# Attention output transposed tile by tile, projection features split and value blocks cleared earlier, and half of one expert weight matrix requested earlier, in a Perceiver block with a mixture of experts

## Chip, cores and metric

The kernel runs on one core of a Trainium2 chip. It is one launch of a program written instruction by instruction for each engine, with semaphores between them. The metric is the device time of one execution in microseconds (us): 675.45 us as the median of 3 runs, from 672.86 to 676.87.

## What is computed

The reference takes 512 tokens (8 sequences of 64, width 512) through three sublayers, each added to x after a layer norm: cross attention to a context of 8 x 512 rows, a linear attention, and a mixture of 16 experts with a shared expert.

```python
x = x + xattn(layernorm(x), ctx, ctx, Wq, bq, Wk, bk, Wv, bv, Wo, bo)      # 16 heads of 32
x = x + attn(layernorm(x), w_qkv, proj_matrix, w_out, b_out)
x = x + ffn(layernorm(x), gate_w, Wg, Wu, Wd, Ws_g, Ws_u, Ws_d)

def attn(x, w_qkv, proj, w_out, b_out):                                    # linear attention
    q, k, v = heads(x @ w_qkv)
    q_proj = elu1(einsum('bhnd,hdf->bhnf', q, proj))                       # elu1(x) = x + 1 if x > 0 else exp(x)
    k_proj = elu1(einsum('bhnd,hdf->bhnf', k, proj))
    kv = einsum('bhnf,bhnd->bhfd', k_proj, v)
    z = 1 / (einsum('bhnf,bhf->bhn', q_proj, k_proj.sum(2)) + 1e-8)
    return merge(einsum('bhnf,bhfd->bhnd', q_proj, kv) * z) @ w_out + b_out

def ffn(h, gate_w, Wg, Wu, Wd, Ws_g, Ws_u, Ws_d):
    scores = softmax(einsum('bsd,ed->bse', h, gate_w)).transpose(0, 2, 1)
    topk_w, topk_idx = top_k(scores, 8)                                    # each expert takes 8 tokens of each sequence
    x_tok = h[topk_idx]
    eo = (gelu(x_tok @ Wg.T) * (x_tok @ Wu.T)) @ Wd.T * topk_w
    return scatter_add(eo, topk_idx) + (gelu(h @ Ws_g.T) * (h @ Ws_u.T)) @ Ws_d.T
```

## The kernel before

Every engine has its own list of instructions, written out in the functions `perceiver_block` defines for SP (the queue of loads), POOL, ACT, DVE and PE. An engine works its list in order; a wait on a semaphore holds back all that stands behind it on that engine. Tokens are in 4 tiles of 128 (`NT`), the width of 512 is in 4 tiles of 128 (`KT`).

**Cross attention** (to about 286 us in the profile) runs over the 8 sequences. Its last sequence overlaps with the output projection (`cross_residual`, L1354) and the layer norm of the linear attention. DVE adds the projection to x (L831), takes the statistics (L812, L813, L814), ACT takes the square root (`ln_std`, L527), DVE finishes with `xn_lin` (L824). ACT does these square roots between its copies of the transposed probabilities (`last_probs_T_out`, L637), in the order of its list. POOL meanwhile subtracts the high part of the weights from the raw ones (`weights_low`, L503: `wlv_lo`, later `wlk_lo`, `wlq_lo`) and clears the block-diagonal value tile `v_bd` (L507, L511).

**Linear attention** (about 286 to 374 us) first projects q, k and v (`qkv_project`, L1405), each product as three of a high and a low part. `proj_hi` (ACT, L680) and `proj_lo` (DVE, L986) are the same split of the feature matrix. The table `LIN_ORDER` then sets the order of all that follows on PE, ACT and DVE: "p" is a projection of q, "k" and "q" are features (L1427, L1433; exponent L689, relu L691, DVE L999), "kv" the products of L1444, and ("att", i, t) is half i of the attention output of token tile t (L1456), which DVE divides and stores in `att` (L1021 to L1027). The last four entries are

```python
        LIN_ORDER += [("att", 1, t) for t in range(NT)]
```

Then PE transposes all of `att` (L1465) into four banks, one for each of the 4 tiles of the width, and ACT copies two of them to `att_T` (L703), DVE the other two (L1035). PE multiplies by `w_out` (`residual`, L1354) when all four copies are there. Behind its copies ACT splits the router's weights and the first stripes of the shared expert (`gate_hi`, `ws_g_hi`, `ws_u_hi`, `ws_d_hi`), DVE subtracts (`gate_lo`, `ws_g_lo`, `ws_u_lo`, `ws_d_lo`, L1048 to L1045), and only then, in DVE's list, come the layer norms of the four tiles (`residual_ln`, L831 first).

**Mixture of experts** (from about 390 us): the router's scores are transposed to [16, 512] in PSUM, copied to SBUF (L1107), and DVE takes the 8 largest of each sequence (L1109) and their positions (L1112). These indices, spread by PE over all partitions (L1594), pick the tokens (L1606, `x_slot`). Then the 24 items of `ITEMS` follow: 16 experts and 8 stripes of the shared expert, in the pattern s, e, e, s, e, e. Each expert has 3 matrices of 2 MB: `w_g`, `w_u` (L1495) and `w_d` (L1532), in two buffers each. SP requests a matrix as soon as PE has used the one that is in its buffer (`expert_load`). `w_d1`, the buffer for the odd experts' down weights, lies over tiles of the routing (`xn_moe`, `spread_i`), so its first load waits for the last pick (`sp.wait_ge(slot_ps, 2 * KT)`).

## Time and profile before

| what | value |
|---|---|
| median of 3 runs | 675.45 us |
| profiled execution, its own time | 672.65 us |
| span of the profiled execution, first to last instruction | 669.5 us |
| mean granted TensorE clock | 0.997 |
| PE busy | 638.5 us, 95% of the span |
| DVE busy | 319.3 us, 48% |
| ACT busy | 254.6 us, 38% |
| POOL busy | 36.6 us, 5% |
| DMA, mean | 193 GB/s, 129.55 MB |

PE is the engine with the most work, but a matmul that is pipelined counts as busy to its modelled end, so the 95% are not all work at full rate. The 31 us that PE is not busy lie in a few places. The timeline names each: a row in it has its start, its length, the engine, the line, what is written and read, and in brackets how long the engine stood idle before the row and who released it.

### The profile page before, as it was taken

Reading aid. Unit: us, or ns where it says so; the run is one execution under the profiler, and the core shown is the slowest. Engines: PE = TensorE matmul, PEld = TensorE weight load, DVE = VectorE, ACT = ScalarE, POOL = GpSimd, SP = SyncE. Lnnn points to the kernel's source line nnn. Section 1 sums busy time; section 2 is a strip of 40 time slices with the busy share of each in tenths; the row PEclk is TensorE's granted clock in tenths of the full one; section 3 lists DMA queues with packets and bytes.
Section 4 is the critical chain, followed back from the end, with each engine's and each line's share of the span. In section 5 each row is a group of like instructions: output and inputs, shape, how many; then the busy total and the mean of one; then the engine's idle time right before and its main releaser. Section 6 shows DMA issues by size and latency. Waiting matters only on the chain.

```text
span 669.5 us, 10402 instructions
## 1 busy us (share of the span) xinstructions
PE 638.5 (95%) x4216; PEld 414.6 (62%) x4216; DVE 319.3 (48%) x646; ACT 254.6 (38%) x486; POOL 36.6 (5%) x38
## 2 busy tenths in 40 slices
PE   6989999999999999898999998999999999999997
PEld 5767777787878776576888565444444434443433
DVE  5964635445362626847778775323233232323123
ACT  5744635454454426437685252111121212211110
POOL 0300000000000002436000000000000000000000
PEclk9999999999999999999999998999999999999999
DMA  8111010110430000030319633989999999999972
GB/s 312 81 64 64 1 65 14 51 62 3 173 143 1 1 2 1 1 111 0 130 57 430 265 130 126 389 334 417 381 415 416 406 399 404 391 380 387 370 291 74
DMA packets 14347, 129.55 MB, mean 193 GB/s; under 512 B 2720, under 2 KB 2848, under 8 KB 6240
## 3 DMA queue, kind: packets, MB, share of 16 engines
q1 hardware_dynamic: 12576, 127.15, 48.7%
q10 hardware_dynamic: 1728, 1.77, 0.8%
q8 instruction: 33, 0.54, 0.3%
q14 instruction: 10, 0.08, 0.0%
HBM read 125.90 MB, written 1.05 MB: 190 GB/s over the span
## 4 chain that ended last, share of the span: by engine, by line
PE 78%; DVE 9%; DMA 5%; ACT 4%; issue 2%; ACTq 2%; SPq 1%; DVEq 0%
PE ps L1211 22%; PE ps L1495 14%; PE ps L1532 7%; PE ps L1505 5%; PE ps L1405 5%; DMA w_u<-in_wu 4%; PE ps L1281 4%; PE ps L1354 3%; PE ps L1545 3%; PE ps L1257 3%; PE ps L1292 2%; PE ps L1322 2%; PE ps L1444 2%; ACTq L396 2%; PE ps L1456 1%
## 5 line engine op out<-in xcount | busy, mean ns | idle before, releaser
L1495 PE MATMUL ps<-w_u,x_slot 128*64 128x512 f32 x256 | 58.1, 595 | 1.3 <-DMA w_u<-in_wu 1.3
L1532 PE MATMUL ps<-w_d,hid_T 128*64 128x512 f32 x256 | 58.2, 596 | 1.1 <-ACT hid_T L763 1.1
L1495 PE MATMUL ps<-w_g,x_slot 128*64 128x512 f32 x256 | 58.1, 595 | 0.8 <-ACT x_slot L779 0.8
L582 ACT ACTIVATE probs<-ps,neg_max 128x512 f32<-128x512 f32 x64 | 43.5, 688 | 39.1 <-DVE neg_max L898 39.1
L741 ACT ACTIVATE hid<-ps 128x512 f32<-128x512 f32 x24 | 14.4, 598 | 102.6 <-PE ps L1495 76.8
L1211 PE MATMUL ps<-wv_hi,ctx_hi 128*128 128x512 f32 x128 | 51.5, 403 | 0.0
L878 DVE COPY probs_T<-ps 128x512 f32<-128x512 f32 x28 | 19.4, 692 | 64.8 <-PE ps L1281 64.8
L1211 PE MATMUL ps<-wv_lo,ctx_hi 128*128 128x512 f32 x128 | 49.9, 390 | 0.0
L1211 PE MATMUL ps<-wv_hi,ctx_lo 128*128 128x512 f32 x128 | 49.8, 389 | 0.0
L898 DVE TENSOR_REDUCE neg_max<-ps 128x1 f32<-128x512 f32 x64 | 39.8, 684 | 18.4 <-PE ps L1257 18.3
L1073 DVE TENSOR_TENSOR hid<-hid,ps 128x512 f32<-128x512 f32 x24 | 16.5, 687 | 65.7 <-PE ps L1495 36.1
L1211 PE MATMUL ps<-ctx_hi,wk_hi 128*128 128x512 f32 x112 | 44.4, 396 | 0.4 <-ACT k_T L567 0.4
L1211 PE MATMUL ps<-ctx_lo,wk_hi 128*128 128x512 f32 x112 | 43.6, 390 | 0.0
L1211 PE MATMUL ps<-ctx_hi,wk_lo 128*128 128x512 f32 x112 | 43.6, 390 | 0.0
L567 ACT ACTIVATE k_T<-ps,bias_k 128x512 f32<-128x512 f32 x32 | 21.6, 688 | 48.8 <-PE ps L1211 48.8
L1532 PEld LDWEIGHTS ps<-w_d,hid_T 128*64 128x64 f32 x256 | 17.7, 137 | 35.7 <-issue 34.4
L1495 PEld LDWEIGHTS ps<-w_u,x_slot 128*64 128x64 f32 x256 | 18.1, 137 | 35.0 <-issue 33.0
L1495 PEld LDWEIGHTS ps<-w_g,x_slot 128*64 128x64 f32 x256 | 17.9, 137 | 35.3 <-issue 34.2
L758 ACT COPY x_slot<-ps 64x512 f32<-64x512 f32 x14 | 8.1, 580 | 76.6 <-PE ps L1532 76.6
L1211 PEld LDWEIGHTS ps<-wv_hi,ctx_hi 128*128 128x128 f32 x128 | 24.0, 188 | 15.9 <-issue 5.7
L891 DVE TENSOR_SCALAR probs<-probs,row_inv 128x512 f32<-128x512 f32 x64 | 31.2, 487 | 2.3
L1281 PE MATMUL ps<-ident,probs 128*128 128x128 f32 x256 | 31.0, 274 | 0.0
(248 smaller groups left out, 1194.2 us busy)
## 6 DMA issues: line engine op xcount, KB each, us to landing
w_u<-in_wu SPq DMA_DIRECT2D x16, 2048.0 KB, 15.5
w_d<-in_wd SPq DMA_DIRECT2D x16, 2048.0 KB, 11.9
w_g<-in_wg SPq DMA_DIRECT2D x16, 2048.0 KB, 13.0
ctx_raw<-in_ctx SPq DMA_DIRECT2D x7, 1024.0 KB, 4.7
w_qkv<-in_wqkv SPq DMA_DIRECT2D x1, 3072.0 KB, 15.1
ws_g<-in_wsg SPq DMA_DIRECT2D x1, 2048.0 KB, 7.7
ws_u<-in_wsu SPq DMA_DIRECT2D x1, 2048.0 KB, 7.6
ws_d<-in_wsd SPq DMA_DIRECT2D x1, 2048.0 KB, 21.0
```

Source lines behind the costliest of these rows:

```text
L567: act.activation(k_T[:, ht, :], bank(FIRST_K + ht if first else PROJ[ht % 2]), ACT.Identity, bias=bias_k[:, ht:ht + 1], scale=1.0).then_in ...
L582: act.activation(probs[:, p, :], bank(SCORE[p]), ACT.Exp, bias=neg_max[:, p:p + 1], scale=1.0, accum_out=row_sum[:, p:p + 1]).then_inc(exp ...
L891: dve.tensor_scalar(probs[:, p, :], probs[:, p, :], row_inv[:, p:p + 1], None, ALU.mult).then_inc(prob_done, 1)
L898: dve.tensor_reduce(neg_max[:, p:p + 1], bank(SCORE[p]), AX.X, ALU.max, negate=True).then_inc(max_done, 1)
L1211: ins = pe.matmul(dst, a(dt), c(dt), start=(dt == 0 and i == 0), stop=(dt == KT - 1 and i == 2))
L1257: ins = pe.matmul(ps[L * side:L * (side + 1), SCORE[2 * ht + j // 2], :], q_T[rows, ht, L * b:L * (b + 1)], k_T[rows, ht, :], start=True, ...
L1281: ins = pe.transpose(ps[:, TRANS[ht % 2][pr], P * st:P * (st + 1)], probs[:, 2 * ht + pr, P * st:P * (st + 1)], ident[:])
L1354: ins = pe.matmul(bank(RES_BANK[k][t]), rows_T[:, dt, P * t:P * (t + 1)], w[:, dt, :], start=(dt == 0), stop=(dt == KT - 1))
L1405: ins = pe.matmul(bank(qkv_bank(n)), a, c, start=(dt == 0 and i == 0), stop=(dt == KT - 1 and i == 2))
L1495: ins = pe.matmul(ps[64 * fh:64 * (fh + 1), dst, :], x_slot[:, e, dt, :], weights[e % 2][:, dt, BANK * fh:BANK * (fh + 1)], start=(dt == 0 ...
L1505: ins = pe.matmul(bank(dst), a, c[:, dt, :], start=(dt == 0 and j == 0), stop=(dt == KT - 1 and j == 2))
L1532: ins = pe.matmul(ps[64 * fh:64 * (fh + 1), 6 + side(n), :], hid_T[:, side(n), j, 64 * fh:64 * (fh + 1)], w_d[e % 2][:, KT * fh + j, :], s ...
```

## The change

There are six edits.

1. POOL clears `v_bd` ahead of the four `wlv_lo` subtractions, not behind them.
2. ACT and DVE split the feature matrix (`proj_hi`, `proj_lo`) ahead of the key halves, not behind them, and POOL adds the bias rows to x only when `proj_lo` is finished.
3. `att` is transposed tile by tile of the tokens. Three tiles go between and behind the last attention products, the fourth behind the first tile's product with `w_out`. ACT makes all four copies to `att_T`, DVE none, and a product with `w_out` waits for its own tile.
4. DVE takes the 8 largest and their positions from PSUM. The copy to SBUF is gone.
5. `spread_i` moves into the memory of `x_slot`. With it gone from there, the second half of `w_d1` is free earlier.
6. The load of the second expert's down weights is in two halves of 1 MB. The second half is requested right behind `w_u` of that expert, the first half after the wait for the picks.

```diff
+        first = ExitStack()
+        spread_i = sb(first, "spread_i", [P, E, SLOTS], F32R)
+        first.close()
         x_slot = sb(moe, "x_slot", [P, E, KT, SLOTS])
...
-        spread_i = sb(route, "spread_i", [P, E, SLOTS], F32R)
...
-        ATT_BANK = (0, 1, 2, 7)
+        ATT_BANK = (7, 2, 3, 5)
...
-        LIN_ORDER += [("att", 1, t) for t in range(NT)]
+        LIN_ORDER += [("att", 1, 0), ("att", 1, 1), ("T", 0, 0), ("att", 1, 2), ("T", 0, 1), ("att", 1, 3), ("T", 0, 2)]
...
             expert_load("u", 1)
+            sp.dma_start(w_d1[:, KT:], wd_d[1][:, KT:]).then_inc(wd_half_in, 16)
             sp.wait_ge(slot_ps, 2 * KT)
-            expert_load("d", 1)
+            sp.dma_start(w_d1[:, :KT], wd_d[1][:, :KT]).then_inc(wd_in[1], 16)
...
-            weights_low(range(4))
             pool.wait_ge(v_ps, B * NS)
             pool.memset(v_bd[:], 0.0).then_inc(vbd_zero, 1)
...
-            weights_low(range(4, 12))
+            weights_low(range(12))
             pool.wait_ge(rows_in, 32)
+            pool.wait_ge(proj_split, 2)
             add_row_bias(1, bout_rows)
...
             values_out(6)
-            for n in range(4):
-                heads_high(n, kl_halves, n)
-                qkv_high((8 + n,))
             act.wait_ge(proj_in, 64)
             for i in range(2):
                 act.activation(proj_hi[:, :, i, :], proj_twice[:], ACT.Identity,
                                scale=head_mask[:, i:i + 1]).then_inc(proj_hi_done, 1)
+            for n in range(4):
+                heads_high(n, kl_halves, n)
+                qkv_high((8 + n,))
             values_out(7)
...
-            for dt in (0, 2):
-                act.wait_ge(attT_ps, dt + 1)
-                act.copy(att_T[:, dt, :], bank(ATT_BANK[dt])).then_inc(attT_act, 1)
+            for t in range(NT):
+                act.wait_ge(attT_ps, t + 1)
+                act.copy(att_T[:, :, P * t:P * (t + 1)],
+                         bank(ATT_BANK[t]).rearrange("p (k c) -> p k c", k=KT)).then_inc(attT_done, 1)
...
-            for dt in (1, 3):
-                dve.wait_ge(attT_ps, dt + 1)
-                dve.tensor_copy(att_T[:, dt, :], bank(ATT_BANK[dt])).then_inc(attT_dve, 1)
...
-            link(dve.tensor_copy(score_T, ps[0:E, 7, :]))
+            scores = ps[0:E, 7, :]
             for b in range(B):
-                ins = dve.max(top_w[:, b, :], score_T[:, L * b:L * (b + 1)])
+                ins = dve.max(top_w[:, b, :], scores[:, L * b:L * (b + 1)])
             link(ins)
             for b in range(B):
-                ins = dve.max_index(top_i[:, b, :], top_w[:, b, :], score_T[:, L * b:L * (b + 1)])
+                ins = dve.max_index(top_i[:, b, :], top_w[:, b, :], scores[:, L * b:L * (b + 1)])
...
+            def att_transpose(t):
+                pe.wait_ge(att_done, NT + t + 1)
+                for dt in range(KT):
+                    ins = pe.transpose(ps[:, ATT_BANK[t], P * dt:P * (dt + 1)], att[:, t, P * dt:P * (dt + 1)], ident[:])
+                ins.then_inc(attT_ps, 1)
...
             for t in range(NT - 1):
+                pe.wait_ge(attT_done, t + 1)
                 residual(1, t, att_T, w_out)
+                if t == 0:
+                    att_transpose(NT - 1)
+            pe.wait_ge(attT_done, NT)
             moe_transpose(0)
```

DVE has the same exchange of `proj_lo` and the key halves as ACT has of `proj_hi`.

PE at the end of the linear attention, before. The row of `kv,q_feat` is the last attention product, `ident,att` are transposes, `w_out,att_T` is the output projection, `ident,xn_moe` transposes for the experts.

```order
L1456 MATMUL ps<-kv,q_feat 128x96 [waits feat_done,att_done,kv_done_dve,kv_done_act]
L1456 MATMUL ps<-kv,q_feat 128x96 x7
L1465 MATMUL ps<-ident,att 128x128 [waits att_done,feat_done]
L1465 MATMUL ps<-ident,att 128x128 x3
L1465 MATMUL ps<-ident,att 128x128 [waits att_done]
L1465 MATMUL ps<-ident,att 128x128 x3
L1465 MATMUL ps<-ident,att 128x128 [waits att_done]
L1465 MATMUL ps<-ident,att 128x128 x3
L1465 MATMUL ps<-ident,att 128x128 [waits att_done]
L1465 MATMUL ps<-ident,att 128x128 x3
L1354 MATMUL ps<-w_out,att_T 128x512 [waits wout_in,attT_dve,attT_act]
L1354 MATMUL ps<-w_out,att_T 128x512 x11
```

The same place in the changed kernel:

```order
L1417 MATMUL ps<-ident,att 128x128 [waits att_done]
L1417 MATMUL ps<-ident,att 128x128 x3
L1465 MATMUL ps<-kv,q_feat 128x96 [waits feat_done,att_done,kv_done_dve,kv_done_act]
L1465 MATMUL ps<-kv,q_feat 128x96 x7
L1417 MATMUL ps<-ident,att 128x128 [waits att_done]
L1417 MATMUL ps<-ident,att 128x128 x3
L1465 MATMUL ps<-kv,q_feat 128x96 [waits feat_done,att_done,kv_done_dve,kv_done_act]
L1465 MATMUL ps<-kv,q_feat 128x96 x7
L1417 MATMUL ps<-ident,att 128x128 [waits att_done]
L1417 MATMUL ps<-ident,att 128x128 x3
L1355 MATMUL ps<-w_out,att_T 128x512 [waits attT_done,wout_in]
L1355 MATMUL ps<-w_out,att_T 128x512 x3
```

The transposes of the first three tiles now stand between or right behind the attention products. Those of the fourth stand behind the 4 matmuls of the first `w_out` product.

ACT at the same place, before:

```order
L691 ACTIVATE relus<-ps 128x512
L703 COPY att_T<-ps 128x512 [waits attT_ps] x2
L719 CAST gate_hi<-gate 128x128 [waits gate_in]
L710 CAST ws_g_hi<-ws_g 128x512 [waits wsd_in,wsu_in,wsg_in]
L711 CAST ws_u_hi<-ws_u 128x512
L716 CAST ws_d_hi<-ws_d 128x512
L527 ACT_TABLE_LOAD
L527 ACTIVATE std<-var_eps 128x1 [waits stats_done] x2
```

and in the changed kernel:

```order
L694 ACTIVATE relus<-ps 128x512
L706 COPY att_T<-ps 128x4x128 [waits attT_ps] x4
L723 CAST gate_hi<-gate 128x128 [waits gate_in]
L714 CAST ws_g_hi<-ws_g 128x512 [waits wsd_in,wsu_in,wsg_in]
L715 CAST ws_u_hi<-ws_u 128x512
L720 CAST ws_d_hi<-ws_d 128x512
L530 ACT_TABLE_LOAD
L530 ACTIVATE std<-var_eps 128x1 [waits stats_done] x2
```

There are four copies instead of two, and `gate_hi` stands behind the fourth.

POOL from the end of the cross attention on, before:

```order
L503 TENSOR_TENSOR wlv_lo<-w_qkv,wlv_hi 128x512 [waits qkv_hi_done] x4
L507 MEMSET v_bd 128x6144 [waits v_ps]
L511 MEMSET v_bd 64x64 [waits vbd_zero]
L511 MEMSET v_bd 64x64
L503 TENSOR_TENSOR wlk_lo<-w_qkv,wlk_hi 128x4x128 [waits qkv_hi_done,vbd_zero]
L503 TENSOR_TENSOR wlk_lo<-w_qkv,wlk_hi 128x4x128 [waits qkv_hi_done] x3
L503 TENSOR_TENSOR wlq_lo<-w_qkv,wlq_hi 128x4x128 [waits qkv_hi_done] x4
L494 TENSOR_TENSOR x<-x,bout_rows 128x512 [waits xn_done,rows_in]
```

and in the changed kernel:

```order
L509 MEMSET v_bd 128x6144 [waits v_ps]
L513 MEMSET v_bd 64x64 [waits vbd_zero]
L513 MEMSET v_bd 64x64
L506 TENSOR_TENSOR wlv_lo<-w_qkv,wlv_hi 128x512 [waits qkv_hi_done,vbd_zero]
L506 TENSOR_TENSOR wlv_lo<-w_qkv,wlv_hi 128x512 [waits qkv_hi_done] x3
L506 TENSOR_TENSOR wlk_lo<-w_qkv,wlk_hi 128x4x128 [waits qkv_hi_done] x4
L506 TENSOR_TENSOR wlq_lo<-w_qkv,wlq_hi 128x4x128 [waits qkv_hi_done] x4
L497 TENSOR_TENSOR x<-x,bout_rows 128x512 [waits xn_done,proj_split,rows_in]
```

The large memset has changed places with the four `wlv_lo`, and the addition of the bias rows waits for `proj_split`.

## Rows read from the trace of the kernel before

**Rows 1.** Busy per stretch: us; PE, PEld, DVE, ACT, POOL; clock, DMA share, GB/s.

```profile
449.96:480.76 30.80, 30.80 (x142) 14.04 (x140) 8.70 (x13) 5.97 (x11) 0.00 (x0) 1.00 0.99 398
```

**Rows 2.** Waits of PE from 420 us on: total, times, longest.

```profile
PE ps L1495 <- DMA w_u<-in_wu: 1.3, 2, 1.1
```

**Rows 3.** Timeline of POOL, 262 to 320 us: start, length, what, idle before it.

```profile
263.89 4.95 POOL L503 TENSOR_TENSOR wlv_lo<-w_qkv,wlv_hi 128x512 fp32r<-128x512 f32 x4 [231.49 <-ACT wlv_hi L642]
268.77 5.26 POOL L507 MEMSET v_bd<- 128x6144 f32 x1
```

**Rows 4.** Timeline of DVE, 262 to 320 us.

```profile
269.27 5.03 DVE L824 TENSOR_SCALAR xn_lin<-x,mean_var,rstd 128x512 f32<-128x512 f32 x1
```

**Rows 5.** Timeline of ACT, 262 to 320 us.

```profile
276.07 0.20 ACT L527 ACTIVATE std<-var_eps 128x1 f32<-128x1 f32 x1 [4.97 <-DVE var_eps L814]
...
279.56 2.03 ACT L637 COPY probs_T<-ps 128x512 f32<-128x512 f32 x4
```

**Rows 6.** Timeline of PE, 262 to 320 us.

```profile
277.38 0.65 PE L1292 MATMUL ps<-probs_T,v_s 128*32 128x64 f32 x32 [2.07 <-ACT probs_T L637]
...
283.19 3.70 PE L1354 MATMUL ps<-w_o,o_T 128*128 128x512 f32 x8 [0.21 <-DVE o_T L883]
```

**Rows 7.** Timelines of DVE and POOL, 0 to 34 us.

```profile
25.03 0.55 DVE L824 TENSOR_SCALAR probs<-x,mean_var,rstd 128x512 f32<-128x512 f32 x1
25.50 5.77 DVE L926 TENSOR_TENSOR wq_lo<-o_T,wq_hi 128x512 fp32r<-128x512 f32 x4
25.74 6.66 POOL L494 TENSOR_TENSOR x<-x,bo_rows 128x512 f32<-128x512 f32 x4 [23.41 <-DVE probs L824]
```

**Rows 8.** Timeline of PE, the first features of the linear attention.

```profile
314.64 0.39 PE L1427 MATMUL ps<-proj_hi,kl_halves 128*128 128x256 f32 x1 [2.27 <-DVE proj_lo L986]
```

**Rows 9.** Timelines of ACT and DVE around the feature matrix's split.

```profile
298.49 1.19 ACT L649 CAST kl_halves<-ps 64x512 fp32r<-64x512 f32 x2 [2.21 <-PE ps L1405]
...
308.58 2.19 ACT L680 ACTIVATE proj_hi<-proj_twice,head_mask 128x1024 fp32r<-128x1024 f32 x2
310.35 4.24 DVE L986 SCALAR_TENSOR_TENSOR proj_lo<-proj_twice,head_mask,proj_hi 128x1024 fp32r<-128x1024 f32 x2
```

**Rows 10.** SP's loads of that matrix, in the timeline and by time to landing.

```profile
288.09 1.82 SPq L435 DMA_DIRECT2D proj_twice<-in_proj  x4
proj_twice<-in_proj SPq DMA_DIRECT2D x4, 128.0 KB, 3.7
```

**Rows 11.** Timeline of PE, end of the linear attention.

```profile
364.50 7.43 PE L1456 MATMUL ps<-kv,q_feat 128*128 128x96 f32 x64 [1.13 <-DVE q_feat L999]
375.37 10.54 PE L1354 MATMUL ps<-w_out,att_T 128*128 128x512 f32 x24 [1.21 <-ACT att_T L703]
```

**Rows 12.** Timeline of DVE, 360 to 412 us.

```profile
372.59 0.86 DVE L1027 TENSOR_TENSOR att<-ps,den_inv 64x256 f32<-64x256 f32 x2
...
376.90 0.69 DVE L1045 TENSOR_TENSOR ws_d_lo<-ws_d,ws_d_hi 128x512 fp32r<-128x512 f32 x1
379.15 0.69 DVE L831 TENSOR_TENSOR x<-ps,x 128x512 f32<-128x512 f32 x1 [1.56 <-PE ps L1354]
...
390.33 0.69 DVE L831 TENSOR_TENSOR x<-ps,x 128x512 f32<-128x512 f32 x1 [0.24 <-PE ps L1354]
```

**Rows 13.** Timeline of ACT, the copies of att_T.

```profile
373.87 1.07 ACT L703 COPY att_T<-ps 128x512 f32<-128x512 f32 x2 [10.64 <-PE ps L1465]
```

**Rows 14.** Timeline of DVE, the softmax of the router and the top 8.

```profile
398.05 0.23 DVE L1101 TENSOR_TENSOR logit<-ps,lmax 128x64 f32<-128x64 f32 x1
...
399.34 0.23 DVE L1105 TENSOR_TENSOR logit<-logit,linv 128x64 f32<-128x64 f32 x1
400.27 0.68 DVE L1107 COPY give<-ps 16x512 f32<-16x512 f32 x1 [0.70 <-PE ps L1588]
```

**Rows 15.** Busy per stretch, columns as in rows 1: the picking.

```profile
404.00:410.00 6.00, 4.87 (x22) 4.08 (x23) 4.14 (x7) 1.92 (x4) 0.00 (x0) 0.72 0.00 0
```

**Rows 16.** Busy per stretch, columns as in rows 1: the queue runs empty.

```profile
446.00:447.00 1.00, 1.00 (x8) 0.32 (x6) 0.00 (x0) 0.47 (x1) 0.00 (x0) 1.00 0.08 33
```

More of the change, by code:

```diff
@@ L268, in perceiver_block @@
         ctx_in, wqkv_in, wo_in, wout_in, rows_in = (sem(f"{n}_in") for n in ("ctx", "wqkv", "wo", "wout", "rows"))
-        proj_in, gate_in = sem("proj_in"), sem("gate_in")
+        proj_in, gate_in, wd_half_in = sem("proj_in"), sem("gate_in"), sem("wd_half_in")
         wg_in, wu_in, wd_in = ([sem(f"{n}_in{i}") for i in range(2)] for n in ("wg", "wu", "wd"))
@@ L295, in perceiver_block @@
         kv_ps, kv_done, att_ps, att_done = sem("kv_ps"), [sem("kv_done_act"), sem("kv_done_dve")], sem("att_ps"), sem("att_done")
-        attT_ps, attT_act, attT_dve = sem("attT_ps"), sem("attT_act"), sem("attT_dve")
+        attT_ps, attT_done = sem("attT_ps"), sem("attT_done")
         logit_ps, lsub_done, lexp_done, score_done = (
@@ L980, in _ @@
             values_out(6)
-            for n in range(4):
-                heads_low(n, kl_halves, n)
-            values_out(7)
             for i in range(2):
@@ L988, in _ @@
                                          op1=ALU.subtract).then_inc(proj_split, 1)
+            for n in range(4):
+                heads_low(n, kl_halves, n)
+            values_out(7)
             u = w = a = 0
@@ L1014, in _ @@
                     w += 1
-                else:
+                elif kind == "att":
                     dve.wait_ge(att_ps, a + 1)
@@ L1411, in _ @@
                     linear_transpose(NT - 1)
+            def att_transpose(t):
[3 more added lines that the diff above has]
+                ins.then_inc(attT_ps, 1)
             u = w = a = 0
             for kind, i, r in LIN_ORDER:
-                if kind == "p":
+                if kind == "T":
+                    att_transpose(r)
+                elif kind == "p":
                     qkv_project(i)
@@ L1460, in _ @@
                     a += 1
-            pe.wait_ge(feat_done, 32)
-            for t in range(NT):
-                pe.wait_ge(att_done, NT + t + 1)
-                for dt in range(KT):
-                    ins = pe.transpose(ps[:, ATT_BANK[dt], P * t:P * (t + 1)], att[:, t, P * dt:P * (dt + 1)], ident[:])
-                    if t == NT - 1:
-                        ins.then_inc(attT_ps, 1)
-            pe.wait_ge(attT_act, 2)
-            pe.wait_ge(attT_dve, 2)
             pe.wait_ge(wout_in, 16)
@@ L1529, in item_down @@
                     pe.wait_ge(wd_in[e % 2], 16 * (e // 2 + 1))
+                    if e == 1:
+                        pe.wait_ge(wd_half_in, 16)
                     for j in range(KT):
```

## Prediction

> **What bounds the kernel now.** I read the busy times by stretch first, then PE's waits, then the timelines around each edited line. In the expert stage PE and the load queue are both full: a pair of experts takes 30.80 us, all of it PE busy, at a DMA share of 0.99 [rows 1], and the loads that PE waits for cost it 1.3 us in all, 1.1 of it at the last `w_u` [rows 2]. All loads there are requested when PE frees a buffer, so if PE comes to the experts earlier, the queue does too. Hence a microsecond won on the path ahead of the experts is a microsecond at the end, and the question is what each edit does to PE's path between 262 and 412 us. There, edits touch four places: a stall of DVE behind POOL, PE's wait for the feature matrix, the change from linear attention to the experts, and the routing.
>
> The profiled execution took 672.65 us, 3.15 more than its span. The sum is made against it; the median of the three runs is 2.8 us higher, and I carry the difference over unchanged.
>
> **Clearing `v_bd` first.** DVE's `xn_lin` of tile 0 took 5.03 us [rows 4], where the same statement elsewhere takes 0.55 [rows 7]. It starts in POOL's 5.26 us memset and ends with it [rows 3]. So DVE is 4.48 late, tile 1's square root runs on ACT at 276.07 after 4.97 idle [rows 5], ACT's copies of the probabilities stand behind it in its list, and PE waits 2.07 for them [rows 6]. In the new order the memset, whose condition (the last values) holds before POOL's first row at 263.89, starts there at the latest and ends by 269.15, before `xn_lin` at 269.27. What runs beside `xn_lin` now are the four `wlv_lo`, 4.95/4 = 1.24 each [rows 3]. A DVE instruction beside such a subtraction is slowed too, but by one at a time: four and four of them alternate in 5.77 and 6.66 us [rows 7], so 0.2 to 1.2 us for each `xn_lin`, and DVE's tile 1 has 1.8 us to spare before ACT's copies are wanted. Followed on, tile 2 is no longer late either, ACT's four copies begin at 276.7 instead of 279.56 [rows 5], and the last `w_o` product starts at 280.5 instead of 283.19 [rows 6]. **Gain 2.7**; at least 2.07 if only the named wait goes, and 0 if the new neighbours hold DVE as long as the memset did (rival c). `wlv_lo` ends near 274.7 and is wanted at 283.6, so its move costs nothing.
>
> The Trainium skill (SBUF — State Buffer, "Who interferes with whom") says that VectorE and GpSimd share a port pair which one instruction holds alone until it ends, a GpSimd operation of any kind holding off a `tensor_scalar` in its two-port mode. By that rule the memset's stall goes, and `xn_lin` may meet at most one `wlv_lo`; rows 4 and 7 agree.
>
> **Splitting the feature matrix first.** PE stands 2.27 us for `proj_lo` at 314.64 [rows 8]. In the new place ACT's 2.19 us of `proj_hi` fit exactly into the 2.21 it stands idle ahead of the first key half at 298.49 [rows 9]. DVE's two `proj_lo` (4.24 together [rows 9], part of which I lay to POOL's bias rows running beside them, which now wait) begin 1.1 us after ACT and end by 300 to 301.6, against a first key half that DVE took at 299.1. It catches up in the 1.4 us gaps behind, and PE needs the key halves at 312 only. The matrix has landed: requested until 289.91, plus 3.7 us, is 293.6 [rows 10], wanted at 296.3. What is late next is ACT, which after its last q half loads the table of Exp; its first exponent comes only 0.5 us earlier, but PE has 12 matmuls of the next projection to do meanwhile. **Gain 2.25** (2.27 less a short wait at the fourth feature); ends 1.7 and 2.3. POOL's added wait delays nobody: the bias rows are wanted 60 us later.
>
> **Transposes by tile.** On PE alone this is a gain. Before, attention products run from 364.50 for 7.43, and the `w_out` products start at 375.37 after 1.21 of waiting [rows 11]. Now three transposes of 0.44 lie between them and the first `w_out` product starts at 373.2; the three products and the fourth transpose end at 384.0 instead of 385.7. But the chain that counts here is not PE's. ACT copies tile 3 only when PE has transposed it, and PE does that behind the first product (10.54/3 = 3.5 us [rows 11]): 373.2 + 3.5 + 0.6 = 377.3. Before, ACT's second copy began at 374.4 [rows 13]. All of ACT's splits stand behind that copy, and DVE's subtractions behind the splits: `ws_d_lo` ended at 377.59 [rows 12], 3.24 after the second copy began. Now it ends at 377.3 + 3.24 = 380.5. Only then may DVE start tile 0's layer norm, at 379.15 before [rows 12]. From there DVE works without a pause, three tiles of 3.43 and one `xn_lo_moe`, to tile 3's row at 390.33, which had waited 0.24 for PE [rows 12]. Now DVE comes to it at 380.5 + 10.9 = 391.4, PE having ended at 389.7. **Loss 1.1.** That DVE no longer copies does not help it, for it waits for ACT. The other end is a gain of 1.6, if tile 0's layer norm followed the first product.
>
> **Top 8 from PSUM.** The copy is 0.68 and its link 0.03, all on the chain to the picks [rows 14]. The 16 instructions behind it now read PSUM. Their price in PSUM is not in the trace; the nearest rows are one subtraction from PSUM and one product from SBUF, both 64 wide and both 0.23 [rows 14]: no extra. I allow 0.1 for all. **Gain 0.6**; ends 0.71 and, should each take half as long again of its 0.14 to 0.2, a loss of 0.6.
>
> The Trainium skill (VectorE: DVE Perf Modes, "The TRN2 errata") gives a VectorE instruction 120 cycles plus its elements from PSUM against 58 from SBUF. At the page's 0.96 GHz that is an estimated 65 ns each, 1.0 for sixteen, and the edit would lose 0.3. Rows 14 show no such difference, but for other operations.
>
> **Half of `w_d1` early.** The queue stands empty before the picks, and 1 MB moves there. But the queue also runs empty at 446 us, with a share of 0.08 [rows 16], behind the load that is shortened. What was saved ahead is idle time there, and the queue's lateness at the end grows only after it. **Gain 0**; at most the 1.1 of rows 2 here. The added wait of PE is for a load that has landed; moving `spread_i` costs no instruction.
>
> **Sum:** 2.7 + 2.25 - 1.1 + 0.6 = 4.45. 672.65 - 4.45 = 668.2 for an execution like the profiled one, and 675.45 - 4.45 = **671.0** as median.
>
> **Rivals.**
> (a) The clock stays up. The picking starts after PE has stood idle for the indices, and from 404 to 410 us the granted clock averages 0.72 [rows 15], a mixture of 2.4 and 1.2 GHz: 6 x 0.28 = 1.7 us lost. The chain ahead is 0.6 shorter, so the idle time is too. If the clock does not fall, up to 1.3 more is won: 669.7. Against it: most of the idle time stays.
> (b) The tile transposes win after all, the layer norms following PE: 1.6 instead of -1.1, 668.3. For it: PE's own rows. Against it: the order of ACT's and DVE's lists.
> (c) POOL does not hand over between its instructions. `xn_lin` waits for all four `wlv_lo`, to 274.7 or, slowed as in rows 7, 275.9. The first part is worth 0 to -1.5, total 673.7 to 675.2. Rows 7 speak against it.
> (d) The top 8 from PSUM cost 0.3 to 0.6: 671.9 to 672.2.
> (e) **Slower:** the queue becomes the bound of the expert stage. A pair needs 12.6 MB in 30.80 us, 408 GB/s, and the queue moved 398 at a full share [rows 1]. From 450 us to the last `w_u` it is never empty, 200 us, so 1% less rate is 2 us more. The point from which it decides is the 1.1 of rows 2, which then grows with all of it; 4% less costs 8 and gives 679. For it: the half load gives no reserve against it, and the runs spread by 4 us. Against it: the change adds no byte and shifts all requests together.
>
> **Chances.** Forecast 0.50, (a) 0.14, (b) 0.10, (c) 0.11, (d) 0.10, (e) 0.05. A measurement can tell about 0.5%, 3.4 us, from no change; so faster means below 672.1. The forecast lies there in four of five draws of its terms (0.40), with (a), (b) and a fifth of (d): 0.66. Within 0.5% lie the rest of it, (c) and most of (d): 0.29. Slower is (e): 0.05. The range takes in the bounds of the first three terms, (a), (d) and the near end of (b): 667.0 to 675.2, leaving out the sums of good ends, and (e).
>
> **What the new profile should show.** `xn_lin` of tile 0 at 0.6 to 1.8 us and no wait of PE for `probs_T`; no wait for `proj_lo`; the fourth `att_T` copy about 4 us after the third, and DVE's first `x` row of the third layer norm straight behind `ws_d_lo`, with no idle time for PE; no copy ahead of the top 8, whose rows keep 0.20; the last `w_u` still waited for by about 1 us. The forecast is wrong if `xn_lin` still takes 4 us, if DVE's layer norm starts before `ws_d_lo` has ended, or if PE's waits for loads in the expert stage exceed 3 us.

## The result, and the profile after

| | before | after |
|---|---|---|
| median of six runs of each, side by side | 674.85 us (672.86 to 677.48) | 667.31 us (665.76 to 669.32) |
| ratio, 95% interval | | 0.9886 (0.9854 to 0.9919) |
| profiled execution, its own time / span | 672.65 / 669.5 us | 665.76 / 664.0 us |
| mean granted clock of that execution | 0.997 | 1.000 |

The change is faster by 7.5 us of medians. The forecast was 671.0, within 667.0 to 675.2, from a sum of 4.45: right in sign and just inside the range, with a gain 3.1 us too small and a time 3.7 us too high.

One reading aid for all comparisons below: the first `x` row behind the first `w_o` product starts at 266.21 us before and at 267.37 after, though no edit lies ahead of it; in the other profiles it lies between 266.4 and 268.3, whatever was edited. I take differences from that row on ("net"). Between these two profiles, 1.09 of the 1.16 arise in the first 20 us: PE's first matmuls of 512 columns take 0.63 us, as they do at half clock behind the wait in u_proj below, and then 0.39; in the profile before 8 of them are slow, in the one after 13. The recorded clock reads 1.00 in this place, so no mean clock below contains it.

**Clearing first.** The timelines of the changed kernel from 262 to 284 us (start, length, engine, what, idle before it), POOL, DVE, ACT, PE:

```profile
263.89 5.23 POOL L509 MEMSET v_bd<- 128x6144 f32 x1 [230.32 <-PE ps L1212]
...
269.73 5.17 POOL L506 TENSOR_TENSOR wlv_lo<-w_qkv,wlv_hi 128x512 fp32r<-128x512 f32 x4
...
270.11 0.93 DVE L827 TENSOR_TENSOR rstd<-rstd,newton 128x1 f32<-128x1 f32 x1
271.07 1.47 DVE L828 TENSOR_SCALAR xn_lin<-x,mean_var,rstd 128x512 f32<-128x512 f32 x1
...
274.30 0.20 ACT L530 ACTIVATE std<-var_eps 128x1 f32<-128x1 f32 x1 [2.06 <-DVE var_eps L818]
...
277.95 2.03 ACT L640 COPY probs_T<-ps 128x512 f32<-128x512 f32 x4
...
275.81 1.10 PE L1293 MATMUL ps<-probs_T,v_s 128*32 128x64 f32 x64
...
281.58 2.84 PE L1355 MATMUL ps<-w_o,o_T 128*128 128x512 f32 x6 [0.21 <-DVE o_T L887]
```

The memset starts where POOL's first row did [rows 3] and is over before `xn_lin`, which takes 1.47 us instead of 5.03 [rows 4]. Two DVE instructions are each stretched once beside `wlv_lo`: `rstd` to 0.93 (0.16 for the next tile) and `xn_lin` to 1.47 (0.55). The 64 matmuls of `probs_T` run in one group without the 2.07 us pause [rows 6]. The last `w_o` product is 14.21 us behind the first `x` row, before 16.98: **2.77 gained**, where 2.7 was forecast.

The Trainium skill (SBUF — State Buffer, "Who interferes with whom") has VectorE and GpSimd hold a shared port pair one instruction at a time; these rows agree: `rstd` took 0.77 us more than for the next tile and `xn_lin` 0.92, each less than one `wlv_lo` of 1.29.

**The feature matrix first.** The same timelines from 290 to 316 us:

```profile
294.57 2.19 ACT L680 ACTIVATE proj_hi<-proj_twice,head_mask 128x1024 fp32r<-128x1024 f32 x2
...
295.75 2.48 DVE L987 SCALAR_TENSOR_TENSOR proj_lo<-proj_twice,head_mask,proj_hi 128x1024 fp32r<-128x1024 f32 x2 [0.97 <-ACT proj_hi L680]
...
310.60 0.28 PE L1436 MATMUL ps<-proj_hi,kl_halves 128*128 128x256 f32 x1
...
315.24 0.39 PE L1436 MATMUL ps<-proj_hi,kl_halves 128*128 128x256 f32 x1 [0.27 <-DVE k_feat L1003]
```

The wait of 2.27 us [rows 8] is gone; 0.27 came back at the fourth feature, a wait that the prediction named but allowed only 0.02 for. The two `proj_lo` take 2.48 instead of 4.24 [rows 9], with POOL's bias rows no longer beside them. From the last `w_o` product to the second half of the attention products PE needs 79.31 us instead of 81.31: **2.0 gained** (2.25 forecast).

**Transposes by tile.** From 360 to 390 us, ACT, DVE, PE:

```profile
369.54 0.58 ACT L706 COPY att_T<-ps 128x512 f32<-128x512 f32 x1 [1.61 <-PE ps L1417]
373.41 0.59 ACT L706 COPY att_T<-ps 128x512 f32<-128x512 f32 x1 [3.29 <-PE ps L1417]
373.89 0.30 ACT L723 CAST gate_hi<-gate 128x128 fp32r<-128x128 f32 x1
...
374.23 0.29 DVE L1049 TENSOR_TENSOR gate_lo<-gate,gate_hi 128x128 fp32r<-128x128 f32 x1 [3.65 <-ACT gate_hi L723]
...
375.95 0.69 DVE L1046 TENSOR_TENSOR ws_d_lo<-ws_d,ws_d_hi 128x512 fp32r<-128x512 f32 x1
376.67 0.69 DVE L835 TENSOR_TENSOR x<-ps,x 128x512 f32<-128x512 f32 x1
...
387.43 0.68 DVE L835 TENSOR_TENSOR x<-ps,x 128x512 f32<-128x512 f32 x1
...
360.89 3.34 PE L1465 MATMUL ps<-kv,q_feat 128*128 128x96 f32 x28 [1.14 <-DVE q_feat L1003]
...
369.34 3.60 PE L1355 MATMUL ps<-w_out,att_T 128*128 128x512 f32 x8
...
383.59 0.66 PE L1475 MATMUL ps<-ident,xn_moe 128*128 128x128 f32 x4 [0.94 <-DVE xn_moe L828]
```

This is the chain of the prediction: ACT's fourth copy 3.87 us after the third, the splits behind it, DVE idle 3.65 us for the first of them, tile 0's row straight behind `ws_d_lo` with no idle time. PE comes to its `w_out` products earlier (8.45 us behind the attention products, before 10.87 [rows 11]) and then waits for DVE three times, 2.3 us in all. Tile 0's row is 15.78 us behind the attention products' start (14.65 before): 1.13 lost; by tile 3 the loss is 26.54 against 25.83, **0.7** (1.1 forecast): DVE now needs 3.38 us a tile instead of 3.43, and no longer waits 0.24 for PE.

**Top 8, the picking, the loads.** DVE's rows, then the busy time of 400 to 406 us (us; PE, PEld, DVE, ACT, POOL; clock, DMA share, GB/s), then PE's waits:

```profile
397.35 1.14 DVE L1110 MAX8 top_w<-ps 16x8 f32<-16x64 f32 x8 [0.70 <-PE ps L1594]
...
398.60 0.21 DVE L1113 FIND_INDEX8 top_i<-top_w,ps 16x8 uint32<-16x64 f32 x1
```

```profile
400.00:406.00 6.00, 4.37 (x29) 3.62 (x29) 4.44 (x10) 2.46 (x5) 0.00 (x0) 1.00 0.00 0
```

```profile
PE ps L1600 <- DVE spread_i L1122: 1.3, 1, 1.3
...
PE ps L1499 <- DMA w_u<-in_wu: 0.4, 1, 0.4
```

The copy is gone, `spread_i` starts 3.55 us earlier than before, tile 3's row 2.90 earlier: **0.65 gained** (0.6). In this stretch the clock was 1.00, where rows 15 had 0.72, and from the first pick to the first expert product PE took 5.04 us instead of 6.24: 1.2 more. Waits for `w_u` fell from 1.3 us [rows 2] to 0.4, and from that product to the end it took 256.22 instead of 256.97.

So the spans differ by 2.77 + 2.0 - 0.7 + 0.65 = 4.7 from the steps, 1.2 from the clock and 0.75 behind the picks, less the 1.16 by which this execution entered later (5.5 in all). The steps are the 4.45 of the forecast. Left open by these two traces: whether the other part is chance, or something that the change buys.

### The profile page after: what moved, and what is told of

It reads as the page before. It is cut to its first block, busy times and chain, and to the rows that moved or that the text cites. A ratio compares the mean times of both kernels' runs of the same rounds, so it can differ in the third digit from the quotient of the medians.

```text
span 664.0 us, 10402 instructions
## 1 busy us (share of the span) xinstructions
PE 637.7 (96%) x4216; PEld 413.5 (62%) x4216; DVE 312.1 (47%) x643; ACT 255.1 (38%) x488; POOL 34.8 (5%) x38
## 4 chain that ended last, share of the span: by engine, by line
PE 76%; DVE 9%; DMA 5%; ACT 5%; issue 2%; ACTq 2%; SPq 1%; DVEq 0%
PE ps L1212 23%; PE ps L1499 14%; PE ps L1538 7%; PE ps L1509 5%; PE ps L1406 5%; PE ps L1282 4%; DMA w_u<-in_wu 4%; PE ps L1551 3%; PE ps L1258 3%; PE ps L1293 2%; PE ps L1323 2%; PE ps L1453 2%; ACTq L398 2%; PE ps L1355 2%; PE ps L1465 1%
```

## The experiments

The runs by kernel; those "before" are the three sets taken with the experiments, whose clocks are on record. "Clock" is the mean over the runs of their mean granted clock, "full" how many had 0.999 or 1.0.

| kernel | median us (runs) | ratio to before, 95% | clock | full |
|---|---|---|---|---|
| before, three sets | 674.2 (43) | | 0.9937 | 0 |
| after, both sets | 667.5 (12) | 0.9886; 0.9898 (0.9876 to 0.9921) | 0.9980 | 4 |
| u_memset | 670.07 (6) | 0.9946 (0.9923 to 0.9968) | 0.9975 | 1 |
| u_proj | 670.81 (10) | 0.9939 (0.9919 to 0.9959) | 0.9964 | 1 |
| u_trans | 667.05 (4) | 0.9893 (0.9857 to 0.9930) | 0.9985 | 2 |
| u_copy | 668.35 (6) | 0.9907 (0.9885 to 0.9929) | 0.9972 | 1 |
| u_half | 666.50 (4) | 0.9890 (0.9856 to 0.9924) | 0.9985 | 2 |
| fix | 664.37 (6) | 0.9842 (0.9816 to 0.9868) | 0.9995 | 6 |
| fixfill | 664.47 (6) | 0.9842 (0.9814 to 0.9870) | 0.9997 | 6 |
| proj_fill | 670.50 (6) | 0.9926 (0.9899 to 0.9952) | 0.9983 | 3 |
| before_fill | 672.57 (12) | 0.9966 (0.9948 to 0.9984) | 0.9964 | 3 |
| before_fill3 | 671.14 (6) | 0.9944 (0.9925 to 0.9964) | 0.9998 | 6 |

**u_memset: the clearing back behind four rows.**

```diff
+            weights_low(range(4))
             pool.wait_ge(v_ps, B * NS)
             pool.memset(v_bd[:], 0.0).then_inc(vbd_zero, 1)
...
-            weights_low(range(12))
+            weights_low(range(4, 12))
```

> The changed kernel with edit 1 alone undone: POOL subtracts the four wlv_lo first and clears v_bd behind them. If the memset is what held DVE, xn_lin of tile 0 takes about 5 us again, PE waits about 2 us for probs_T, and the last w_o product starts 2.8 us later against the end of the last values; the time is about 670.0. Rival: the stall is worth nothing downstream since PE has slack, or POOL's subtractions hold DVE as long: then within 0.5 us of 667.3.

Measured 670.07, 2.6 above the changed kernel. Timelines of DVE and PE, then the busy time of a stretch (columns as above):

```profile
270.41 5.03 DVE L829 TENSOR_SCALAR xn_lin<-x,mean_var,rstd 128x512 f32<-128x512 f32 x1
...
278.51 0.87 PE L1294 MATMUL ps<-probs_T,v_s 128*32 128x64 f32 x32 [2.07 <-ACT probs_T L641]
```

```profile
278.00:282.00 4.00, 3.49 (x45) 3.35 (x46) 3.42 (x12) 1.63 (x4) 0.00 (x0) 0.60 0.00 0
```

The 5.03 us and the 2.07 us are back to the digit. New is the clock behind the wait: 0.60 over 4 us, where the profile of the kernel before has 1.00. In this profile the last attention products are 3.55 late (net), 2.77 of it the steps and 0.8 the clock, while the picking ran at 1.00.

**u_proj: the split back behind the key halves.**

```diff
-            act.wait_ge(proj_in, 64)
-            for i in range(2):
-                act.activation(proj_hi[:, :, i, :], proj_twice[:], ACT.Identity,
-                               scale=head_mask[:, i:i + 1]).then_inc(proj_hi_done, 1)
             for n in range(4):
                 heads_high(n, kl_halves, n)
                 qkv_high((8 + n,))
+            act.wait_ge(proj_in, 64)
+            for i in range(2):
+                act.activation(proj_hi[:, :, i, :], proj_twice[:], ACT.Identity,
+                               scale=head_mask[:, i:i + 1]).then_inc(proj_hi_done, 1)
```

(on DVE likewise, and POOL's wait taken out)

> The changed kernel with edit 2 alone undone: proj_hi and proj_lo behind the key halves, and the bias rows do not wait for them. The theory expects PE's wait for proj_lo of 2.3 us back, the first feature 2.0 to 2.3 us later, and a time of about 669.4. Rival: ACT's table load and exponents bound the first features anyway, then under 1 us.

Measured 670.81: 3.3 to 3.5 above the changed kernel where 2.1 was expected. PE's timeline and the stretch behind the wait:

```profile
313.25 0.38 PE L1435 MATMUL ps<-proj_hi,kl_halves 128*128 128x256 f32 x1 [2.27 <-DVE proj_lo L989]
...
314.96 0.63 PE L1405 MATMUL ps<-xn_lo,wlq_hi 128*128 128x512 f32 x1
```

```profile
314.00:318.00 4.00, 4.00 (x14) 3.27 (x14) 2.54 (x4) 1.58 (x3) 1.57 (x2) 0.57 0.35 82
392.00:396.00 4.00, 3.85 (x14) 2.90 (x15) 3.37 (x10) 0.21 (x2) 0.00 (x0) 0.57 0.36 150
```

The first feature is 2.43 late (net), but the attention products 3.53: matmuls of 0.39 us take 0.63 behind the wait, in a stretch of some 3.4 us at half clock. In this execution a wait of 2 us cost 3.5. The second row above is another such stretch, from 392.5, behind waits for `xn_moe` and `xn_hi` of 0.95, 1.01 and 0.77 us; it cost 1.0 more up to `spread_i`, so short waits in a row can have one behind them too. From this came the theory of the clock: each of PE's waits of some 2 us brings, in many executions, such a stretch, and the profile that the forecast was made from, faster than the three runs beside it, had only one while PE was at work, in the picking. The 43 runs of the kernel before agree: span and mean clock go together (correlation -0.84), 4.6 us for 0.01. A stretch of 3.4 us at half clock takes 1.7/670 = 0.0025 from the mean, so by this slope it costs 1.2 us (0.8 to 1.4 in the rows of the profiles), and the kernel before has on average two to three of them in a run (1 - 0.9937), the changed one not quite one.

**u_trans: the transposes as they were** (all of PE's at the end, ACT and DVE two copies each).

```diff
-        LIN_ORDER += [("att", 1, 0), ("att", 1, 1), ("T", 0, 0), ("att", 1, 2), ("T", 0, 1), ("att", 1, 3), ("T", 0, 2)]
+        LIN_ORDER += [("att", 1, t) for t in range(NT)]
...
-                pe.wait_ge(attT_done, t + 1)
                 residual(1, t, att_T, w_out)
-                if t == 0:
-                    att_transpose(NT - 1)
```

> The changed kernel with edit 3 alone undone: all transposes behind the attention products, two copies of att_T on ACT and two on DVE. If the chain through ACT's fourth copy and the splits behind it is what sets the third layer norm, this kernel is 0.7 to 1.1 us faster than the changed one, about 666.4, with DVE's first x row of the third layer norm 14.6 us behind the start of the last attention products, as before. Rival: PE's order decides, then it is 1.6 us slower, about 668.9.

Measured 667.05, 0.3 to 0.4 below the changed kernel: too small for these runs, the rows decide. DVE's first and last `x` row, and the picking:

```profile
375.27 0.69 DVE L834 TENSOR_TENSOR x<-ps,x 128x512 f32<-128x512 f32 x1 [1.56 <-PE ps L1357]
...
386.45 0.69 DVE L834 TENSOR_TENSOR x<-ps,x 128x512 f32<-128x512 f32 x1 [0.24 <-PE ps L1357]
```

```profile
400.00:406.00 6.00, 5.24 (x24) 4.60 (x25) 3.56 (x6) 2.28 (x5) 0.00 (x0) 0.72 0.00 0
```

Tile 3's row is 0.7 earlier than in the changed kernel (net), with DVE waiting for PE again. So this edit loses 0.7 by itself. The profiled execution is longer all the same, 666.0 against 664.0: the clock fell in the picking (1.44 lost up to the first expert product) and its waits for `w_u` were 2.4 us instead of 0.4.

**u_copy: the copy back ahead of the top 8.**

```diff
-            scores = ps[0:E, 7, :]
+            link(dve.tensor_copy(score_T, ps[0:E, 7, :]))
+            scores = score_T
```

> The changed kernel with edit 4 undone: DVE copies the scores from PSUM to SBUF ahead of the top 8 again (0.68 and a link of 0.03), and the 16 instructions behind it read SBUF. If reading PSUM costs them 0.00 to 0.04 us more each, as MAX8 x8 showed (1.14 against 1.10), spread_i starts 0.6 later and the median is 0.6 above the changed kernel's. If the errata's 62 more cycles for each of them held, the copy would be the better form and the time 0.3 lower. Either is at the edge of what five rounds tell; the rows decide: MAX8 x8 at 1.10, FIND_INDEX8 at 0.20, start of spread_i.

Measured 668.35, 0.75 above the changed kernel's 667.6 in the same set. DVE's rows:

```profile
397.46 0.68 DVE L1108 COPY give<-ps 16x512 f32<-16x512 f32 x1 [0.70 <-PE ps L1595]
398.17 1.10 DVE L1111 MAX8 top_w<-give 16x8 f32<-16x64 f32 x8
...
399.38 0.21 DVE L1114 FIND_INDEX8 top_i<-top_w,give 16x8 uint32<-16x64 f32 x1
```

Eight MAX8 take 1.10 us from SBUF and 1.14 from PSUM, a FIND_INDEX8 0.20 to 0.21 from either; `spread_i` starts 0.68 later (net). The extra cycles in the expectation are those of the Trainium skill (VectorE: DVE Perf Modes, "The TRN2 errata"); for these two operations no run here shows them, and the measurement decides.

**u_half: the second expert's load in one piece again.**

```diff
-            sp.dma_start(w_d1[:, KT:], wd_d[1][:, KT:]).then_inc(wd_half_in, 16)
             sp.wait_ge(slot_ps, 2 * KT)
-            sp.dma_start(w_d1[:, :KT], wd_d[1][:, :KT]).then_inc(wd_in[1], 16)
+            expert_load("d", 1)
```

> The changed kernel with edit 6 alone undone: w_d1 in one load behind the picks. If the queue runs empty again before the experts' steady part, nothing changes: 667.3 within 0.7 us, and the wait of PE for the last w_u stays between 0.3 and 1.3 us. Rival: the 1 MB is a reserve that is still there at the end; then PE's waits for loads grow by up to 2.6 us and the time is up to 669.9.

Measured 666.50, not above the changed kernel. The half load buys nothing that four runs show.

**fix: ACT's fourth copy behind the splits.** A version that the chain above suggests.

```diff
-            for t in range(NT):
...
+            def att_T_out(tiles):
...
+            att_T_out(range(NT - 1))
...
             shared_high_gu(0)
             shared_high_d(0)
+            att_T_out((NT - 1,))
```

> The changed kernel with ACT's list altered at one place: the fourth att_T copy stands behind the copies of gate_hi and the ws_*_hi, no longer ahead of them. Theory of the list order (edit 3 loses because these splits wait behind the fourth copy): DVE's ws_d_lo ends before PE's first w_out product does, DVE's first x row of the third layer norm follows that product, some 3 us earlier than 376.67, and tile 3's row comes 2.3 to 2.7 us earlier than 387.43; the time falls from 667.3 by as much, to 664.6 to 665.0. Rival (the loss lies with PE's order or with DVE): x rows where they are, 667.3. Second rival (the load queue is the bound from here on): rows earlier, but PE's waits for loads grow from 0.4 us by the same 2.5, 667.3.

Measured 664.37, the fastest kernel here, 3 us below the changed one. ACT and DVE, then PE's waits:

```profile
370.09 0.30 ACT L726 CAST gate_hi<-gate 128x128 fp32r<-128x128 f32 x1
...
373.48 0.59 ACT L707 COPY att_T<-ps 128x512 f32<-128x512 f32 x1 [1.53 <-PE ps L1421]
...
373.12 0.69 DVE L839 TENSOR_TENSOR x<-ps,x 128x512 f32<-128x512 f32 x1 [0.27 <-PE ps L1359]
...
384.73 0.69 DVE L839 TENSOR_TENSOR x<-ps,x 128x512 f32<-128x512 f32 x1 [0.24 <-PE ps L1359]
```

```profile
PE ps L1503 <- DMA w_u<-in_wu: 1.8, 2, 0.9
```

The splits fill the gap in which ACT waited for the fourth transpose, the copy starts no later, tile 0's row follows the first product, and tile 3's comes 2.7 us earlier: the transposes by tile are now a gain of 2. Two things differ from the expectation. The span fell by 1.6 only against the profile after, because PE waited 2.1 us for loads instead of 0.4; the load queue took 1.1 back, part of what the second rival said. And all six runs had the full clock, against 4 of 12, which is where the median got the rest. PE's three waits for `xn_moe`, 2.3 us in all, are down to 0.2. That these brought low stretches on is likely: the wait for `spread_i` is as long as before (1.28), and the second stretch of u_proj lies behind them. No run isolates it.

**fixfill: the kernel fix with matmuls in what is left of the wait for `spread_i`.** Their results are overwritten.

```diff
             item_value(0)
+            for _ in range(5):
+                pe.matmul(bank(4), ones[:], xn_hi[:, 0, :], start=True, stop=True)
```

> The kernel fix with five added matmuls of 512 columns on PE, into a bank that is overwritten next, between item_value(0) and the wait for the first half of spread_i. Theory of the clock (a wait of PE costs more than its length because in many executions the granted clock falls to half behind it for about 3.4 us): the added matmuls take 1.2 us of a wait that is there anyway, no run has a low stretch in the picking, and the median falls against fix by what such stretches cost it, 0.5 to 1.2 us: about 664.0. Rival (the clock plays no part in the medians): as fix, within 0.2. If the added matmuls reach beyond the wait: up to 0.5 slower than fix.

Measured 664.47, as fix; the fall of 0.5 to 1.2 that was expected did not come. This tells nothing on the theory, since fix had no low stretch to remove.

**proj_fill: u_proj with matmuls inside the wait.**

```diff
                     if u == 0:
+                        qkv_out(5)
+                        for _ in range(8):
+                            pe.matmul(bank(5), ones[:], xn_hi[:, 0, :], start=True, stop=True)
                         pe.wait_ge(proj_split, 2)
```

> The changed kernel with edit 2 undone (PE waits 2.27 us for proj_lo again) and eight added matmuls of 512 columns into a free bank inside that wait, which stays. Clock theory: the stretch at half clock behind the wait, 313.95 to 317.3 us in the profile without edit 2, is gone in every run, and the median of 670.8 falls by 1.1 to 1.5, to 669.3 to 669.7, which is the changed kernel plus the 2.0 of the wait itself. Rival (edit 2's 3.5 us are a wait and something else that it moved on ACT, DVE or POOL): 670.8 as without the added matmuls.

Measured 670.50: the time missed, 0.3 below u_proj and not 1.1 to 1.5. PE's timeline and two stretches:

```profile
311.55 2.03 PE L1429 MATMUL ps<-xn_hi,ones 128*128 128x512 f32 x8
314.01 0.39 PE L1438 MATMUL ps<-proj_hi,kl_halves 128*128 128x256 f32 x1 [0.43 <-DVE proj_lo L989]
```

```profile
314.00:318.00 4.00, 3.99 (x22) 3.46 (x23) 3.30 (x5) 1.81 (x4) 2.35 (x2) 1.00 0.30 66
406.00:411.00 5.00, 5.00 (x31) 5.00 (x30) 2.20 (x4) 2.94 (x6) 0.00 (x0) 0.66 0.00 0
```

Behind the filled wait the clock is 1.00 and the attention products are 2.05 late (net), not 3.53, which is the wait alone. But this execution lost 1.4 in the picking instead, and its waits for loads were 3.0 us. Over the runs the mean clock rose, from 0.9964 to 0.9983, which by the slope above is 0.9 us; the medians differ by 0.3, too little for six and ten runs to tell. So the next two fill more places.

**before_fill and before_fill3: the kernel before, its waits filled; and the changed kernel once more.** The first has the eight matmuls at `proj_lo` and five at `spread_i`; the second eight at each, and eight more in the wait for `probs_T`:

```diff
             attend(B - 1, 0)
+            for _ in range(8):
+                pe.matmul(bank(RES_BANK[0][3]), ones[:], xn_hi[:, 0, :], start=True, stop=True)
             attend(B - 1, 1)
```

> The kernel before, with the eight added matmuls in the wait for proj_lo and the five in the wait for spread_i, nothing else altered; all waits keep their length. Clock theory: the kernel before loses 2 to 3 us more in its median than in its fastest execution through such stretches; with two of its three places filled the median comes to 672.0 to 673.0 (from 674.3 to 674.9), ratio 0.9965 to 0.998, and the mean clocks of its runs rise from .990 to .997 to .997 and 1.0. Rival (clock no part of it): ratio 1.000.

Measured 672.57, 1.4 faster than before and inside the expected 672.0 to 673.0. The clocks missed: 0.997 to 1.0 was expected, and seven of the twelve runs had 0.994 or 0.995. The profile shows two low stretches, one at `probs_T`, which was not filled, and one in the picking, where the five matmuls had left 0.75 us of the wait:

```profile
278.00:282.00 4.00, 3.73 (x48) 3.67 (x49) 3.42 (x10) 1.72 (x5) 0.00 (x0) 0.63 0.00 0
406.73 1.10 PE L1599 MATMUL ps<-spread_i,ones 16*128 16x512 f32 x2 [0.75 <-DVE spread_i L1121]
408.00:413.00 5.00, 4.92 (x28) 4.93 (x29) 2.10 (x5) 2.93 (x5) 0.00 (x0) 0.66 0.01 3
```

So five were not enough in this place; the next run has eight, which leave nothing of this wait.

> The kernel before with added matmuls of 512 columns in all three of PE's waits of some 2 us: eight ahead of the second half of the last two attention products (probs_T), eight ahead of the wait for proj_lo, eight ahead of the wait for spread_i. All other work and the waits' ends stay. Clock theory: mean clock .998 to 1.0 in nearly all runs, median 671.0 to 672.0, ratio 0.9955 to 0.997 against before, about 1 us below before_fill (672.6), and 4.7 above the changed kernel. Rival (clock no part of it, or low stretches come as often elsewhere): mean clock .992 to .995 as before and a ratio of 1.000.

Measured 671.14, 3.8 faster than the 674.95 of the kernel before in its set (ratio 0.9944, a little more than the 0.9955 to 0.997 expected). One of the filled waits, and three stretches of before_fill3:

```profile
276.38 2.12 PE L1372 MATMUL ps<-xn_hi,ones 128*128 128x512 f32 x8
278.52 0.65 PE L1292 MATMUL ps<-probs_T,v_s 128*32 128x64 f32 x32
```

```profile
278.00:282.00 4.00, 3.98 (x67) 3.32 (x68) 3.42 (x12) 1.78 (x5) 0.00 (x0) 1.00 0.00 0
314.00:318.00 4.00, 3.57 (x19) 2.76 (x19) 3.35 (x4) 3.41 (x6) 4.00 (x3) 1.00 0.00 0
406.00:412.00 6.00, 5.38 (x35) 4.36 (x34) 4.24 (x8) 3.15 (x6) 0.15 (x1) 1.00 0.00 0
```

Up to the picking nothing comes earlier than in the profile of the kernel before (the last attention products 98.46 us behind the first `x` row, before 98.29), and the waits end when they ended; only the clock differs: 0.999 to 1.0 in all six runs, against none of 43, and the six lie within 1 us. That settles the cause: the low stretches depend on the idle time in these three waits. Their cost is less certain: 3.8 us against the set beside it (2.4 to 5.1 by the interval), 3.1 against the 674.2 of all 43 runs, 2.8 by the slope.

> The changed kernel as it is, timed again so that it stands in one set of runs with the next two. All runs of the other kernels so far put one hundredth of mean granted clock at 4.6 us of span in the kernel before (32 runs), so at equal clock the change should give what the steps on the path came to in the two traces, 4.7 us, and the rest of the 6.7 to 7.5 between the medians should lie in the mean clock: .997 to 1.0 here, .990 to .997 before. Median 666.5 to 667.8. If instead runs of equal clock are 6.5 us or more apart, the clock is not the missing part.

Measured 667.60, mean clock 0.998, two runs of six at 1.0. The picking in this profile:

```profile
402.00:408.00 6.00, 5.41 (x32) 5.19 (x31) 2.82 (x5) 3.42 (x6) 0.53 (x1) 0.72 0.00 0
```

The four runs of the changed kernel at full clock have 665.76 to 666.86, median 666.1. Against before_fill3 that is 5.0 us at equal clock: the 4.7 of the steps, and 0.3 within the spread. The changed kernel loses 667.5 - 666.1 = 1.4 to the clock, the one before 3.8 (or 3.1): 2.4 (or 1.7) less. 5.0 and 2.4 add up to the difference of the medians by the way they were taken, so the sum is no test; the test is that the 5.0 agree with the 4.7 of the rows.

## Why the prediction was right, and where it fell short

- **The steps.** Forecast 2.7, 2.25, -1.1, 0.6 and 0; the two traces have 2.77, 2.0, -0.7, 0.65 and nothing for the half load: 4.7 for 4.45. The chain of the transposes (fourth copy, splits, `ws_d_lo`, layer norm) went row by row as written, only 0.4 cheaper at tile 3. Rivals (b), (c) and (d) are out: the layer norms did not follow PE, POOL handed over between its subtractions, and PSUM cost the sixteen instructions about 0.08 together (3.31 us from the first MAX8 to `spread_i`, 3.23 from SBUF).
- **The step that failed** is "the median of the three runs is 2.8 us higher, and I carry the difference over unchanged". That distance is no constant. By the mean clocks, the profiled execution had one low stretch and a run of the kernel before has two or three on average, and the change takes two of the three waits away and shortens the third. The slope of the 43 runs puts an execution at 0.997 at 672.7, which is where the profiled one lay. By spans it was luckier still: its 3.15 us outside the span are more than any other run here shows (1.75 to 3.01). In which waits the median run had its stretches no trace shows. A wait was priced at its own length, and the three together cost 2.8 to 3.8 us more than that. Not evenly: undone alone, the first edit cost 2.6 in the median, no more than its rows, the second 3.3 to 3.5.
- **Rival (a)** was this mechanism, but priced at the picking alone (1.3) and at a chance of 0.14. It belonged to all three waits: 2.4 of the 3.7 us by which 671.0 was too high, or 1.7 by all 43 runs. The rest: 0.25 from the terms, 0.6 because the kernel before took 674.85 beside the changed one, not the 675.45 that was used, and 0.4 to 1.1 that these runs cannot place. The time lies only 0.3 us inside the lower end of the range, so that the range held it is in part luck.
- **Rival (e)** did not come. But the queue is near: waits for loads ranged from 0 to 3.0 us over the profiles, with no order by edit that I can see, and in fix they took back 1.1 of 2.7. What sets them from run to run stays open.

## What to carry to other kernels

Price a wait of TensorE in mid-kernel at its length and at the granted clock behind it, and read the mean clock of all runs, not of the profiled one: if it is below 1.0 where nothing else differs, filling the waits with matmuls into a free bank shows what the clock is worth, provided that little of a wait is left (0.75 us was too much in before_fill). When a copy is split by tile, look at what stands behind the last piece in that engine's list, and put independent work ahead of it. A result that the next engine reads once and in small pieces may be read from PSUM directly.

## What the hardware showed that I had not expected

- A wait of TensorE of 2.07 to 2.27 us is followed in some executions, not in all, by a stretch of some 3.4 us at 1.2 GHz instead of 2.4, although the engine works again: 0.60 and 0.57 at the waits of u_memset and u_proj, and 1.00 at the same two waits in the profile of the kernel before.
- Even the wait for `spread_i` of 1.3 us, next to shorter ones, did it: granted clock 1.00 in the first profile of the changed kernel and 0.72 in the second, at the same rows (first pick to first expert product 5.04 and 6.47 us).
- At the start of every profile 6 to 13 matmuls of 512 columns take 0.63 us before they take 0.39, while the recorded clock reads 1.00: the mean granted clock does not show this stretch, and its length moved the whole kernel by about 1 us between two profiles.
- A VectorE instruction of one element per lane can be held as well: `rstd` took 0.93 instead of 0.16 us beside a GpSimd subtraction. The instruction ahead of it, `newton` of the same size, took its usual 0.15 beside the same subtraction.
